# Three-layer graph network on one core: one middle pass over four output blocks instead of two over two, column chunks of 512, 512 and 336, and VectorE forming the combined adjacency operands

## The reference

```python
def _gc(x, adj, W, b):
    return adj @ (x @ W) + b
h = relu(layernorm(x))                       # jnp.maximum(_layernorm(x), 0)
h = relu(_gc(h, adj, W1, b1))
h = relu(_gc(h, adj, W2, b2))
out = x + _gc(h, adj, W3, b3)
```

## Time and profile before

| | us |
|---|---|
| median of 3 runs | 1771.65 (1770.06 to 1772.67) |
| the profiled execution's own time | 1772.66 |
| its span, first to last instruction | 1770.8 |
| PE busy | 1655.2 |
| DVE, ACT, POOL busy | 1000.6, 749.1, 533.7 |
| mean granted clock of TensorE | 0.986 |

### The profile page before, as it was taken

How to read it: one execution, slowest core, us unless ns; L and a number is a source line. 1 busy time by engine, 2 the same in 40 slices (tenths; PEclk the granted TensorE clock), 3 DMA queues, 4 the chain that set the end, 5 groups by cost and what they waited for, 6 DMA issues and landing times. The chain is left out here.

```text
span 1770.8 us, 22422 instructions
## 1 busy us (share of the span) xinstructions
PE 1655.2 (93%) x7668; PEld 1444.3 (82%) x7668; DVE 1000.6 (57%) x1581; ACT 749.1 (42%) x1428; POOL 533.7 (30%) x651
## 2 busy tenths in 40 slices
PE   6889999999998999988999987999999999999997
PEld 6778999978787878766888876788998888989896
DVE  5554332245476566666657667565544546766664
ACT  3332221145354444555544444535334544444442
POOL 6786545213144454000005153061000422110202
PEclk9999999999999999999999999999999999999998
DMA  5557676443278889777778888787545335787774
GB/s 189 179 194 263 214 226 199 134 132 97 82 223 276 288 266 299 231 220 228 222 235 281 260 276 253 233 261 248 152 139 164 91 88 155 204 252 212 246 211 149
DMA packets 229686, 366.18 MB, mean 207 GB/s; under 512 B 26000, under 2 KB 207464, under 8 KB 229572
## 3 DMA queue, kind: packets, MB, share of 16 engines
q1 hardware_dynamic: 192222, 279.04, 52.5%
q0 software_dynamic: 13440, 46.66, 7.9%
q10 hardware_dynamic: 23910, 39.05, 6.1%
HBM read 277.30 MB, written 87.19 MB: 206 GB/s over the span
## 5 line engine op out<-in xcount | busy, mean ns | idle before, releaser
L1113 DVE TENSOR_TENSOR ring<-raw,ring 128x452 fp32r<-128x452 f32 (+1 forms) x816 | 567.5, 714 | 374.8 <-ACT ring L926 370.2
L926 ACT CAST ring<-raw 128x452 fp32r<-128x452 f32 (+1 forms) x816 | 457.6, 572 | 528.8 <-PE ps L1427 242.2
L1425 PE MATMUL ps<-ring,S 128*128 128x452 f32 x1596 | 603.7, 378 | 64.9 <-DVE ring L1113 60.5
L1426 PE MATMUL ps<-ring,S 128*128 128x452 f32 x1596 | 592.2, 371 | 0.0
L1427 PE MATMUL ps<-ring,S 128*128 128x452 f32 x1596 | 591.9, 371 | 0.0
L1425 PEld LDWEIGHTS ps<-ring,S 128*128 128x128 f32 x1596 | 302.6, 190 | 133.5 <-DVE ring L1113 86.3
L1427 PEld LDWEIGHTS ps<-ring,S 128*128 128x128 f32 x1596 | 302.6, 190 | 30.5
L1426 PEld LDWEIGHTS ps<-ring,S 128*128 128x128 f32 x1596 | 303.0, 190 | 28.4
L1425 PE MATMUL ps<-slots,still 128*128 128x452 f32 x504 | 190.2, 377 | 30.5 <-DVE still L1076 26.6
L1426 PE MATMUL ps<-slots,still 128*128 128x452 f32 x504 | 187.4, 372 | 0.0
L1427 PE MATMUL ps<-slots,still 128*128 128x452 f32 x504 | 186.7, 370 | 0.0
(11 more groups left out here) (122 smaller groups left out, 1723.6 us busy)
## 6 DMA issues: line engine op xcount, KB each, us to landing
raw<-TS SPq DMA_DIRECT2D x360, 226.0 KB, 3.2
raw<-adjT SPq DMA_DIRECT2D x306, 226.0 KB, 3.6
raw<-adjT SPq DMA_DIRECT2D x63, 452.0 KB, 4.4
TS<-made SPq DMA_DIRECT2D x30, 904.0 KB, 5.9
P<-parts ACTq DMA_DIRECT2D x48, 226.0 KB, 3.8
prep<-P POOLq DMA_DIRECT2D x48, 226.0 KB, 5.3
T<-prep POOLq DMA_DIRECT2D x48, 226.0 KB, 4.4
raw<-T SPq DMA_DIRECT2D x48, 226.0 KB, 3.1
```

What stands on the lines that cost most here:

```text
L926: act.copy(hi, src).then_inc(hi_done, 1)
L1113: dve.tensor_tensor(lo, src, hi.bitcast(F32), ALU.subtract).then_inc(lo_done, 1)
L1425: pe.matmul(out, st_hi, mv_hi, start=start, stop=False)
L1426: pe.matmul(out, st_hi, mv_lo, start=False, stop=False)
```

## The change

- The two middle passes become one (`pass2`): each moving tile serves four output blocks, 12 matmuls. Its stationaries are 512 wide; the sets of two parts are kept at a time (`odd`, `even`), and the set of part i + 1 is loaded (kind `s`) during part i. The running sums are kept on chip in `U` and `V` for all chunks, since the loop is now part by part with the chunks inside. The left-over product of part 4 (part None before) runs inside the next group (`inner`).
- The columns are cut into chunks of 512, 512 and 336 (`WIDTH`) in all passes and in w2; HALF is 1360. The number of matmuls stays the same.
- In the first pass x is loaded straight into the place of its low part (`xin`), without the three `xs` buffers, so its loads wait for no buffer. DVE forms the four combined adjacency tiles (`make`) and does the small steps of the normalisation, both of which POOL did. There are 2 slots (`RING1`) instead of 3. `TS` is laid out by row and part.
- In h1, POOL forms the combined stationaries from `pair_buf` (`combine1`) and stores them to `HS`; ACT stores X22 there. H1B and S2B are gone, and with them the ten uses of `prep_stationary` for h1; the eight for W2 become four of `prep_w2`, 512 wide, and are reloaded 512 wide.
- P2 and H2 and pass3 work as before, on the new widths.

```diff
-W = 452
+WIDTH = (512, 512, 336)
+START = (0, 512, 1024)
 CHUNKS = 3
-HALF = W * CHUNKS
+HALF = sum(WIDTH)
 NP = 2 * HALF
...
-RING1 = 3
-XS = 3
+RING1 = 2
+STAGES = 6
+PAIR_BUFS = 3
+INNER = 5
...
+    def pass2():
+        last_of = {}
+
+        def load_h1(part, t):
+            j = p.tile("s", False)
...
+        leftover = None
+        for part in range(7):
+            if part == 0:
+                extra = []
+            elif part < 6:
+                extra = [lambda t=t, i=part + 1: load_h1(i, t) for t in ORDER]
+            else:
+                extra = [lambda q=q, i=i: load_w2(i, q) for i in (X11, X12, S2) for q in range(4)]
+            half = {1: 0, 5: 0, 6: 1}.get(part)
+            for c in range(CHUNKS):
+                first = 4 * (at["rotation"] % 2)
+                at["rotation"] += 1
+                g = p.group("pass2", c, part, [first + m for m in range(4)])
+                if leftover:
+                    g.inner = p.group("pass2", leftover.chunk, None, leftover.banks)
+                    leftover = None
+                for i, t in enumerate(ORDER):
+                    j = p.tile("moving", True)
+                    j.chunk, j.part, j.pair = c, part, t
+                    g.tiles.append(j)
+                    p.release(j, g, half is None and i == PAIRS - 1)
+                    last_of[part, t] = j.freed
+                    p.emit_due()
+                    if g.inner and i == 0:
+                        tail_step(g.inner, g.inner.chunk, 1)
...
+                        tail_step(g, c, half)
+                    n = c * PAIRS + i
+                    if n % 3 == 1 if part < 6 else n > 3 and n % 2 == 0:
+                        spread_in(extra)
...
+    odd = place("odd", [P, PAIRS, 2, F], F32R, 0)
+    even = place("even", [P, PAIRS, 2, F], F32R, HALF_ROWS)
+    V = place("V", [P, KF, HALF], F32, 2 * HALF_ROWS)
+    U = place("U", [P, KF, HALF], F32, 2 * HALF_ROWS + KF * HALF * 4)
...
             def load_x(q):
-                n, b = q.n, q.block
+                b = q.block
                 if b == SHORT:
+                    sp.wait_ge(rep_zeroed, 1)
                     for r in range(3):
                         sp.dma_start(rep[r * STEP:r * STEP + TAIL, :], x[b * P:N, :]).then_inc(rep_in, 16)
                     return
-                if n >= XS:
-                    sp.wait_ge(lo1_done, xs1[n - XS].ready)
-                sp.dma_start(xs[:, n % XS, :], x[b * P:(b + 1) * P, :]).then_inc(x_in[n % XS], 16)
+                sp.dma_start(xin[:, b, 1, :], x[b * P:(b + 1) * P, :]).then_inc(x_in[b], 16)
 
             def store_made(i):
                 t = ORDER[i % PAIRS]
                 c = i // PAIRS
                 sp.wait_ge(made_done, 4 * (i + 1))
-                sp.dma_start(TS[t, c, :, :], made[:, i % 2, :, :].rearrange("p a w -> p (a w)")) \
-                    .then_inc(made_stored[i % 2], 16)
+                sp.dma_start(TS[t, :, :, within(c)], made[:, i % 2, :, 0:WIDTH[c]]).then_inc(made_stored[i % 2], 16)
 
...
+            def make(i, which):
+
+                c, n = divmod(i, PAIRS)
+                w = WIDTH[c]
+                a, b = chunks1[c][2 * n], chunks1[c][2 * n + 1]
+                Y11, Y12 = (raw1[:, a.raw % RAW1, k, 0:w] for k in range(2))
+                Y21, Y22 = (raw1[:, b.raw % RAW1, k, 0:w] for k in range(2))
+                T2_, T3_, T1_, T4_ = (made[:, i % 2, k, 0:w] for k in range(4))
+                if which == 0:
+                    if i >= 2:
+                        dve.wait_ge(made_stored[i % 2], 16 * (i // 2))
+                    dve.wait_ge(raw1_in[b.raw % RAW1], 16 * (b.raw // RAW1 + 1))
+                    dve.tensor_tensor(T1_, Y12, Y11, ALU.subtract).then_inc(made_done, 1)
+                    dve.tensor_tensor(T3_, Y22, Y12, ALU.subtract).then_inc(made_done, 1)
+                else:
+                    dve.wait_ge(made_done, 4 * i + 1)
+                    dve.tensor_tensor(T2_, Y22, T1_, ALU.subtract).then_inc(made_done, 1)
+                    dve.wait_ge(made_done, 4 * i + 3)
+                    dve.tensor_tensor(T4_, Y21, T2_, ALU.subtract).then_inc(made_done, 1)
...
+                    if j.kind == ("x" if j.chunk is None else "adj") and (j.kind == "x" or j.chunk > 0):
+                        c = j.chunk or 0
+                        if j.n < 2 * PAIRS and j.n % 2 == 1:
+                            make(c * PAIRS + j.n // 2, 0)
+                        elif 0 < j.n <= 2 * PAIRS and j.n % 2 == 0:
+                            make(c * PAIRS + j.n // 2 - 1, 1)
...
+                    if part == 1 and c == 0:
+                        for i in range(PAIR_BUFS):
+                            dve.wait_ge(sums_stored[i], 2 * kept[i])
+                    for m in range(KF):
+                        bank = ps[:, g.banks[m], 0:WIDTH[c]]
+                        u, v = U[:, m, within(c)], V[:, m, within(c)]
+                        if busy and busy[m]:
+                            dve.wait_ge(e_stored[bufs[m][1]], busy[m])
+                        if part == 1 or part == 2:
+                            dve.wait_ge(copied, plan.copied_of["pass2", c, m])
+                        if part != 1:
+                            dve.wait_ge(drained, plan.chain_before["pass2", c, m, part])
+                        dve.wait_ge(group_done, g.done[m])
+                        if part == 1:
+                            dve.tensor_tensor(e(bufs[m][1], c), bank, u, ALU.add).then_inc(drained, 1)
+                        elif part == 3:
+                            dve.tensor_tensor(v, bank, u, ALU.add).then_inc(drained, 1)
+                        elif part == 4:
+                            dve.tensor_tensor(u, bank, u, ALU.add).then_inc(drained, 1)
+                            dve.tensor_tensor(e(bufs[m][1], c), bank, v, ALU.add).then_inc(drained, 1)
+                        elif part is None:
+                            staged = e(bufs[m][1], c)
+                            dve.tensor_tensor(staged, bank, staged, ALU.add).then_inc(drained, 1)
+                        elif part == 5:
+                            dve.tensor_tensor(v, bank, v, ALU.add).then_inc(drained, 1)
+                        else:
+                            dve.tensor_tensor(u, bank, u, ALU.add).then_inc(drained, 1)
...
+            def combine1(pair, turn, stat, n):
+
+                i = turn % PAIR_BUFS
+                A, B = pair_buf[:, i, 0, :], pair_buf[:, i, 1, :]
+                a1, a2, z1, z2 = A[:, 0:F], A[:, F:H], B[:, 0:F], B[:, F:H]
+                pool.wait_ge(kept_stored[i], 16 * (turn // PAIR_BUFS + 1))
+                pool.tensor_tensor(z2, a2, z2, ALU.add).then_inc(combined, 1)
+                pool.wait_ge(combined, n + 1)
+                pool.wait_ge(stat_lo, stat - 1)
+                pool.tensor_tensor(a2, a1, a2, ALU.subtract).then_inc(combined, 1)
+                pool.wait_ge(combined, n + 2)
+                pool.tensor_tensor(a1, z2, a1, ALU.subtract).then_inc(combined, 1)
+                pool.wait_ge(stat_lo, stat)
+                pool.wait_ge(combined, n + 3)
+                pool.tensor_tensor(z1, z1, a1, ALU.subtract).then_inc(combined, 1)
+                pool.dma_start(HS[pair, 0:2, :, :].rearrange("s p f -> p s f"),
+                               A.rearrange("p (s f) -> p s f", s=2)).then_inc(sums_stored[i], 16)
+                pool.wait_ge(combined, n + 4)
+                pool.dma_start(HS[pair, 2:4, :, :].rearrange("s p f -> p s f"),
+                               B.rearrange("p (s f) -> p s f", s=2)).then_inc(sums_stored[i], 16)
...
+            def pass2_group(g):
+                w = WIDTH[g.chunk]
+                part = h1_stat(g.part)
                 for n, j in enumerate(g.tiles):
-                    if first:
-                        pe.wait_ge(stat_lo, plan.stat_of[phase, j.pair, j.part])
+                    if g.chunk == 0 and g.part in (X11, X12):
+                        pe.wait_ge(stat_lo, plan.stat_of["h1", j.pair, g.part])
                     pe.wait_ge(lo_done, j.cut + 1)
                     s = j.slot % RING
+                    end = g.left is None and n == PAIRS - 1
+                    for m in range(KF):
+                        cols = slice(m * P, (m + 1) * P)
+                        if n == 0:
+                            bank_free(g, m)
+                        mm = three(ps[:, g.banks[m], 0:w], part[:, j.pair, 0, cols], part[:, j.pair, 1, cols],
+                                   ring[:, s, 0, 0:w], ring[:, s, 1, 0:w], start=n == 0, stop=end)
...
```

1327 lines of the change are left out of this document (677 added, 650 removed).

## The result

The changed kernel takes 1643.8 us (median, 1639.9 to 1648.7), beside 1770.9 for the kernel before, measured beside it: a ratio of 0.929, 95% interval 0.925 to 0.933. The forecast was 1645 in a range of 1620 to 1693. The profiled run took 1645.5, its span is 1643.6. A second measurement gave 1644.0 against 1770.9 (0.9285, 0.9267 to 0.9303).

The account below looks back on a forecast made before the run. The kernel was taken as bound by PE: its matmuls' own time plus its gaps. Matmuls 1576.5, start 13, losses 15, 2, 6, 7, 1 and 12, tail 11 gave 1643.5, plus 1.9 around it: 1645 us, range 1620 to 1693.

Parts of the forecast that it names:

- Part 1, joined middle passes: Middle passes: each moving tile feeds 12 matmuls instead of 6, leaving 6 us of 98 us loss: -92 us.
- the middle stall stays, because the landing time, not the rate, fed it: Rival for the middle passes: landing time fed the stall, so half of 98 us comes back: 1688 us; chance 0.03.
- Part 2, widths: Chunks of 512, 512 and 336 columns: PE's matmul work becomes 1576.5 us against 1597, -20.5 us.
- the step with three rivals: Price of a 336-column matmul in all passes and w2: 156 ns taken, 152 to 158 ns given.
- The line holds: Rival for 336-column matmuls: the straight line through 452 and 512 columns gives 168 ns, +26 us: 1671 us; chance 0.12.
- the load is the bound: Rival for 336-column matmuls: the weight load sets their distance, 204 ns, +106 us: 1751 us; chance 0.07.
- the rival that forecast a slower kernel: Rival for 336-wide stretches: short matmuls don't hold the clock and cost 280 ns, +273 us: 1918 us; chance 0.02.
- Part 3, the first pass: First pass: x's loads wait for no buffer and POOL leaves; end at 339 us against 359, loss -17 us.
- the mechanism of chunk 0: First pass, chunk 0: PE at 5.41 us per block sets the pace, barely, over DVE at 5.15 us.
- the chunk changes: First pass: PE loses about 4.3 us from chunk 0 to 1 and 3 us from 1 to 2.
- the transition to h1: End of the first pass: one landing, one cast and one cut as before, 2.7 us.
- Part 4, the rest: After the middle passes and in h1: losses of 2 us in h1, 7 in w2, 12 in pass3; tail 11 us.

Follow-up runs that it names:

- e4_drain: Changed kernel with the PSUM drain of a first-pass chunk placed after the cut of the next chunk's block 0 instead of block 1; 1633.2 us, ratio 0.923.

## Why the prediction was right, and where it was not

The sum, term by term, against the profiled run (the losses are the length of a stage in the table less its matmuls at 226.7 and 153.4 ns):

| term | predicted | measured |
|---|---|---|
| matmuls | 1576.5 | 1576.7 |
| first matmul | 13 | 13.5 |
| first pass, loss | 15 | 27.3 |
| h1, loss | 2 | 2.6 |
| middle pass, loss | 6 | 2.3 |
| w2 and w3, loss | 7 + 1 | 3.6 + 0 |
| pass3, loss | 12 | 10.9 |
| after the last matmul | 11 | 6.7 |
| span | 1643.5 | 1643.6 |

That the sum is right to 0.1 us is luck: the first pass cost 12.3 us more and the start, h1 and the matmuls 1.3, and five smaller terms gave 13.5 back.

**Part 1, joined middle passes: right in size, wrong in what fed the loss.** -92 predicted; the joining alone took 95 (the run at width 452). DVE's work per group was estimated at 12.5 of 27 us, 46%; it is 252 of 551, 46%. But the text read the DMA engines, "80% busy", as the cause, and put the DMA share after at 0.45; it is 0.57, and at 0.79 the pass runs as fast. Halving the bytes in the old kernel gave back 20 of 98 us. The stall was the turn of five landing buffers, 6.0 us against the 5.1 that PE's pace allowed, with hardly any slack in it (0.24 us, and 5.05 after joining). Traffic enters by the length of a landing, which is why halving it helped a little. The rows for it had been there: ACT waited for landings, with five buffers in the kernel's text and 273 tiles to count. The rival "the middle stall stays, because the landing time, not the rate, fed it" had the cause right and the result wrong: since a tile now feeds 12 matmuls, the turn may take 9.6 us.

**Part 2, widths: right, with two errors that cancel.** The price of 336 columns was the step with three rivals; 153.4 ns was measured for 156, inside the stated 152 to 158. "The line holds" (168) and "the load is the bound" (204) are out, the latter although the load's records still last about 190 ns: they are longer than the distance of two matmuls, so their length isn't a price. The prediction's own argument from the earlier trace rows was weaker than it reads: that the first matmul "had begun 0.11 after its load" is inferred, since the trace records it at 601.52, together with its load. The Trainium skill ("TensorE: Matmul & The Clock Gate", section "LDWEIGHTS (loading the stationary operand)"), by which a load of 128 columns takes 107 ns, is not contradicted by any run here: the shortest distance of two matmuls, each with its load, is 153 ns. 512 columns cost 226.7 ns and not 225.6: the 399 matmuls of the earlier trace rows include those cut off at the ends of the stretch (no matmul record is missing: both traces have all 7668). That made 5464 x 1.1 = +6, and 336 made 2204 x 2.6 = -6. The granted clock was 1.00 through the middle pass, w2 and pass3, with their 336-wide stretches. In the first pass's 336-wide chunk it was 0.95, but 1.00 in `e4_drain`, where only PE's waits at its start are gone; so the rival that forecast a slower kernel found nothing. Of the widths' whole effect, 28 us, 20.5 were forecast. The same ends of stretches had made 452 too cheap: by the distance of starts it cost 204.8 and 206.6 ns before, and 206.6 throughout in the changed kernel, so that the matmuls alone give 6612 x 206.6 - 4408 x 226.7 - 2204 x 153.4 ns = 29 us. Beside that w2 lost some 9 us instead of 3.6 and the first pass a few less.

**Part 3, the first pass: the mechanism of chunk 0 was right, the rest under-sized.** Its start and loss were to shrink by 17 us, from 45.5, and shrank by 5, to 13.5 + 27.3; its end was to come 20 us earlier, at 339, and came 8 earlier, at 351.5. PE sets the pace of chunk 0, 5.44 us per block for 5.41 predicted, and no wait for x is left; with the wait put back most blocks take 6.2 us and more. What failed is the sentence that made POOL's leaving a relief alone. It priced `make` on DVE (1.2 us a block, 1.4 measured) but not what waits for it: SP's refills of the landing buffers. With `make` in DVE's order they went out late, ACT waited 35.9 us for landings in chunk 1, blocks 9 to 18 of it took 5.5 to 6.0 us (15 to 18 in the second profile), and the chunk 5.6 more than with `make` on POOL. The second term are the chunk changes, 4.3 and 3 predicted: block 0 of the new chunk alone lost 3.5 and 4.2, and the drain placed one block earlier gave 10.8 back. The third are the ends of the chunks, for which the sum has no term but the transition to h1, 2.7: the last two blocks of the three chunks lost 3.5, 6.1 and 4.9 us, over half of the 27.3. The two edits of the first pass together leave 5.5 of these 14.5; the gap before h1 is 4.4 and becomes 2.9.

**Part 4, the rest.** w2 and pass3 came out as worked out, within 3.4 and 1.1 us. pass3's waits were expected in its 336-wide chunk; the longest, 2.9 us of 7.0, is at its start. After the last matmul 6.7 us were needed and not 11: after the last store's issue the span goes on for 3.2 us, where it was 7.6. With the chunks at 452 in the changed kernel the time after the last matmul is 7.4, so the width is not the reason for most of it, and no run tells what is.

## What to carry to other kernels

Count a ring of landing buffers as a loop: buffers times the time that compute takes per tile must exceed landing, casts, cuts and the queues between them; the share of busy DMA engines does not tell it (0.80 stalled, 0.79 did not), and traffic counts by what it adds to a landing. The sign in a trace is how long a landed tile lies before it is used: 0.24 us in the pass that stalled, 5.05 in the one that did not. When an operation moves to another engine, ask first who waits for its result and what stands before it in the new engine's order; its own duration was the smaller part here. A queue's total of waits is no price, though: SP waited as long in the faster kernel. And place the drain of a finished chunk ahead of work for later blocks: one step of order was worth 10.8 us.

## What the runs showed of the hardware

The distance of two matmuls at the granted clock of 1.00 is not the columns' time plus one constant: the extra is 13.4 ns at 336 and at 512 columns, about 15 at 364, 17 at 480, and 16 to 19 at 448, 452 and 464, in the same stream of loads and matmuls. It even differs between stages for one width (448: 202.5 ns in w2, about 206 in the middle pass). Of a landing of 3.6 to 4.0 us only 0.6 to 0.7 went with half of its bytes, while the same 256 KB landed in 2.7 and 2.9 us at a DMA share of 0.57 and in 4.1 and 4.5 at 0.79. And DVE's cut of 2 x 512 columns took 1.23 us with POOL idle and 1.58 with POOL forming operands.
